# One more small TensorE product per item in the edge loop of a graph-attention and mixture-of-experts kernel

## What is computed

```python
def _L0_gnn_ref(feat, e_pro, mask, W_n, attn_l, attn_r, attn_m, src, dst):
    feat_src = (feat @ W_n).reshape(N, H, D)                 # H = 8 heads, D = 32
    el = jnp.einsum('nhd,hdt->nht', feat_src, attn_l)        # T = 4
    er = jnp.einsum('nhd,hdt->nht', feat_src, attn_r)
    em = jnp.einsum('ef,hft->eht', e_pro, attn_m)
    left = jnp.einsum('eht,et->eh', el[src], mask)
    right = jnp.einsum('eht,et->eh', er[dst], mask)
    em_e = jnp.einsum('eht,et->eh', em, mask)
    e = (left + right + em_e) / 3.0
    e = jnp.where(e > 0, e, NEG_SLOPE * e)
    ...
    e_exp = jnp.exp(e - e_max[dst])
    a = e_exp / e_sum[dst]
    msg = feat_src[src] * a[:, :, None]
    rst = jax.ops.segment_sum(msg, dst, num_segments=N)
```

## Time and profile before

| | |
|---|---|
| median of 3 runs | 4229.73 us (4228.48 to 4230.96) |
| the profiled execution | 4242.61 us, span 4240.8 us |
| TensorE matmul busy | 3155.8 us (74%) |
| TensorE weight loads busy | 2393.4 us (56%) |
| VectorE busy | 1982.3 us (47%) |
| ScalarE busy | 1615.5 us (38%) |
| GpSimd busy | 1861.5 us (44%) |
| granted TensorE clock, mean | 0.771 |

### The profile page before, as it was taken

How to read it: one execution, slowest core, us unless ns; L and a number is a source line. 1 busy time by engine, 2 the same in 40 slices (tenths; PEclk the granted TensorE clock), 3 DMA queues, 4 the chain that set the end, 5 groups by cost and what they waited for, 6 DMA issues and landing times. The chain is left out here.

```text
span 4240.8 us, 66247 instructions
## 1 busy us (share of the span) xinstructions
PE 3155.8 (74%) x12650; PEld 2393.4 (56%) x12651; DVE 1982.3 (47%) x5336; ACT 1615.5 (38%) x3611; POOL 1861.5 (44%) x1906
## 2 busy tenths in 40 slices
PE   2532787777777777777777777777766699999997
PEld 1221665555565656555555665565555477777775
DVE  5730555555555555555555555555744122222221
ACT  2311544444444444444444444444422122222221
POOL 0005455556555555555555555555245111111111
PEclk9865667777767777777777677767755899999998
DMA  7744444444444444444444444446553321221113
GB/s 217 253 134 120 122 128 124 125 127 126 125 125 127 128 123 127 131 128 126 125 127 124 125 125 125 125 125 118 87 176 133 101 32 30 32 31 31 31 31 82
DMA packets 311626, 480.40 MB, mean 113 GB/s; under 512 B 164215, under 2 KB 239811, under 8 KB 302670
## 3 DMA queue, kind: packets, MB, share of 16 engines
q0 software_dynamic: 100848, 285.40, 27.4%
q1 hardware_dynamic: 208606, 193.39, 15.2%
q10 hardware_dynamic: 2000, 0.06, 0.0%
HBM read 408.92 MB, written 76.12 MB: 114 GB/s over the span
## 5 line engine op out<-in xcount | busy, mean ns | idle before, releaser
L838 POOL DMA_INDIRECT rows<-table,idx x1664 | 1577.9, 948 | 1141.0 <-issue 488.8
L881 PE MATMUL ps_acc<-rows,hot 128*128 128x264 f32 x3328 | 1274.3, 521 | 396.9 <-DVE acc L1169 342.9
L881 PEld LDWEIGHTS ps_acc<-rows,hot 128*128 128x128 f32 x3328 | 767.9, 255 | 535.1 <-issue 422.0
L1169 DVE TENSOR_TENSOR acc<-acc,ps_acc 128x264 f32 x832 | 356.7, 429 | 1047.0 <-remote 459.5
L866 PEld LDWEIGHTS ps_term<-er,hot_t 128*128 128x128 f32 x3328 | 619.1, 249 | 285.6 <-issue 235.6
L866 PE MATMUL ps_term<-er,hot_t 128*128 x3328 | 608.2, 314 | 125.6 <-issue 93.3
L1155 DVE TENSOR_TENSOR rows<-rows,ps_p 128x512 f32<-128x512 f32 x832 | 565.7, 680 | 2.4 <-ACT ps_p L984 0.5
L973 ACT ACTIVATE hot<-iota_row,neg_rel 128x128 f32<-128x128 f32 x1664 | 545.8, 388 | 4.8 <-PE ps_acc L881 4.6
L1713 PE MATMUL ps_h<-w,acc 128*128 x1680 | 530.8, 459 | 0.5 <-ACT acc L1632 0.5
L1625 POOL DMA_INDIRECT x_dram<-acc,to x105 | 161.8, 1541 | 755.2 <-ACT acc L1641 755.2
L948 ACT COPY e_t<-ps_e 128x128 f32<-128x128 f32 x208 | 57.5, 277 | 1003.1 <-remote 684.3
(11 more groups left out here) (264 smaller groups left out, 2960.7 us busy)
## 6 DMA issues: line engine op xcount, KB each, us to landing
dst_row<-rel_d SPq DMA_DIRECT2D x52, 1024.0 KB
rows<-table,idx POOLq DMA_INDIRECT x1664
rec<-rec_d SPq DMA_DIRECT2D x848, 24.0 KB
rec_d<-acc SPq DMA_DIRECT2D x16, 1050.0 KB
acc<-slots_x SPq DMA_DIRECT2D x105, 130.0 KB, 2.1
acc<-in_edge_attr_dram SPq DMA_DIRECT2D x16, 700.0 KB
wrow<-in_L_ffn_w_dram SPq DMA_DIRECT2D x16, 640.0 KB
table<-fo SPq DMA_DIRECT2D x49, 148.0 KB
```

Of the source, the lines that this page charges most:

```text
L838: pool.indirect_dma_start(rows[w][:, t, :], None, table, bass.IndirectOffsetOnAxis(ap=idx[w][:, t:t + 1], axis=0)).then_inc(gathered[w * Q ...
L881: last = pe.matmul(ps_acc[m % 2][:, 0:PW], hot[m // QI % 2][:, m % QI * G + j, :], rows[m // NI][:, tile_of(m % NI, j), 0:PW], start=(j == ...
L1169: dve.tensor_tensor(so_far, so_far, ps_acc[m % 2][:, 0:PW].rearrange("p (h d) -> p h d", h=HEADS), ALU.add).then_inc(added, 1)
```

## The change

In sums, the wait for added comes first, and after it one more matmul is issued: 104 columns of the constant bm against the identity, into columns 264 to 367 of the item's bank, which nobody reads. Then come the waits for msg_ok and hot_ok and the two products as before, which write columns 0 to 263. The new matmul has no signal of its own. exp_ok is still waited for ahead of it.

```diff
+SPIN = 104
...
                         k1 = i * (2 * NI) + (at + 1)
                         if m % NI == 0:
                             pe.wait_ge(exp_ok, i * 2 + (at // NI + 1))
+
+                        after(pe, added, k1 - 2)
+                        pe.matmul(ps_acc[m % 2][:, PW:PW + SPIN], ident[:, :], flat(bm[:, :, :])[:, 0:SPIN], start=True, stop=True)
                         pe.wait_ge(msg_ok, k1)
                         pe.wait_ge(hot_ok, i * (2 * QUADS) + (at // QI + 1))
-
-                        after(pe, added, k1 - 2)
                         for j in range(G):
```

## The result

The changed kernel takes 4276.35 us (median of 4 runs, 4266.88 to 4277.6) against 4229.77 us before: 46.6 us more, a ratio of 1.0105 with the 95% interval 1.0089 to 1.0121. It is slower, and the forecast had it 18 us faster. The profiled execution took 4276.3 us, with a span of 4274.6.

What follows compares the result with a forecast made beforehand. The prediction took a ring of handshakes in the edge loop, with no engine full, to bound the kernel. Products at +66 us and the clock at -84 us gave net -18 us: 4211.7 us as a median, range 4120 to 4320.

Steps and rivals of the forecast that it cites:

- What bounds the kernel: In the edge loop no engine is full; a ring of handshakes, with TensorE's signals late while gathers stream, sets the pace.
- The moved wait at nothing: Before the sums in the edge loop, moving the wait for added ahead of msg_ok and hot_ok costs nothing by itself.
- The price of a product: On TensorE in the edge loop, each added product takes 0.22 us at full rate and 0.50 at half.
- The clock: In the edge loop TensorE's mean granted clock rises by 0.12, from 0.73 to 0.85, giving -84 us.
- The pass-through of 0.26: In the edge loop 0.26 of added TensorE time lengthens a turn; 253 us of products thus cost +66 us.
- 70 us for 0.10 of clock: Over the edge loop's 26 turns, a mean TensorE clock higher by 0.10 saves 70 us.
- Rival A: In the edge loop the clock rises to 0.99 and pays in full: -134 us, 4095.7 us; chance 0.10.
- Rival B: In the edge loop the clock stays at 0.73 and the products cost +80 us: 4309.7 us; chance 0.19.
- Rival C: In the edge loop a late sum signal makes GpSimd pause 2.78 us once a turn: +65 us, 4276.7 us; chance 0.17.
- Rival D: In the edge loop a clock gain of -63 us and product costs of +69 us nearly cancel: 4235.7 us; chance 0.18.
- Range and chances: For the whole kernel, 4120 to 4320 us; chances 0.46 faster, 0.18 the same, 0.36 slower.

## Why the prediction was wrong, point by point

**What bounds the kernel.** Right in that nothing is full and that the gathers of GpSimd pace the loop; its idle time before them grew from 1023.8 to 1041.3 us in 2500 us. That signals of TensorE are late because gathers are streaming, as the prediction put it, was not shown (last section).

**The moved wait at nothing.** Right (1.0001).

**The price of a product.** Right at half rate (0.53 us against 0.50), too low at full rate (0.28 us against 0.22). The prediction let the weight loads set the pace, as for few columns; 8 columns do take 0.22 us at full rate, 104 take more. At the measured clock of 0.78 this moves the mean from 0.343 to 0.391 us. The 356 ns of a pass of L880 are longer than that because passes overlap.

**The clock.** Mis-sized: +0.05 in place of +0.12. By the prediction's own prices this is the largest part of the miss, 49 of the 65 us between -18 and +46.6. The product comes behind the add, as the prediction said, so the silences remain, and the clock still falls to half rate: in the 24 turns of the changed kernel 22 idle stretches of TensorE are longer than 4 us, the granted clock just before them was 1.00, and after 20 of them TensorE resumed at half rate. Nor was 0.73 the lower bound of the mean, as the prediction had it: with 8 columns it fell to 0.61.

**The pass-through of 0.26, and 70 us for 0.10 of clock.** This is the step that failed in its mechanism. It came from five turns of one trace, and it took for a cause what only went along. The wait moved alone had a trace with more TensorE time a turn (79.7 us) and a lower clock (0.70) than the profile of before has over its 24 turns (76.9 us, 0.73), at 102.17 us a turn against 102.63; with 8 columns, 16.8 us more of TensorE cost 0.39 us. Inserted at 0.78, the formula gives 0.56 x 0.22 + 0.44 x 0.50 = 0.343 us, 832 x 0.343 x 0.26 = +74, less 0.5 x 70 = 35: +39 us, close to the 46.6 measured. That is no proof of it: with 0.70, the clock of the trace with the wait moved alone, in the place of before's 0.73, the same formula gives +18 us; the clock term measured 8 to 15 us for 0.10 (104 against 8 columns) and not 70; and the price of a product isn't even. Slower turns in the earlier trace rows had more TensorE time and a lower clock; that they were slower because of it was argued, and the runs speak against it. Repeated runs of the kernel before don't settle it: in one long sitting its 23 runs show no relation of time and clock, in a short one the longer of its 19 runs tend to have the lower clocks, and which follows from which can't be told.

**What the runs put in its place.** There is slack, and the slack has an end. In long sittings the ratios by products per batch are 1.0004 (4), 1.0006 and 1.0020 (8), 1.0032 (12, without the score quad), 1.0164 (12, without the items 0 to 3), 1.0105, 1.0097 and 1.0155 (16), 1.0104 (24, none in the score quad); in short ones 0.9989 (12), 1.0093 (16, behind all waits), 1.0213 (32). So a measurement of half of such a change would have called it free. In short sittings the loss goes with TensorE's busy time beyond the slack, and a product that delays its sum by 0.05 to 0.07 us instead of 0.28 to 0.53 is free (bfloat16, 1.0013). In long sittings, where the forecast was made and missed, busy time alone costs next to nothing (the wait moved alone, 8 against 104 columns), and the products cost what no single quantity read here explains. Why is open, and so is why the products of the score quad would need the others to become dear: its chain steps grow by the same 0.4 us where only its own products are there and nothing is lost.

**Rival A** fell with the clock. **Rival B**, the clock stays, was too strict: it rose by 0.05; the silences remained and the mean stayed below 0.8. The rule of the Trainium skill that an idle stretch of TensorE between bursts puts the clock back to half (TensorE: Matmul & The Clock Gate, HAM oscillation) agrees with that: it did so after 20 of the 22. But its price of 80 us rested on the same 0.26. **Rival C** named 4276.7 us, and 4276.35 came out. Its mark was there too, GpSimd's waits above 566 us although the clock rose, but it is no mark of the loss: with the products at the items 8 to 11 alone they are 605 us, and nothing is lost. Its place was not: the products at places 3 and 0 of a quad, which delay just the sum that it named, cost 0.20% alone. And its number was the sum of a clock gain that hardly exists (8 to 15 us for 0.10, as above) and a pause that was only supposed, so the agreement is an accident. **Rival D**, a wash at +0.09 of clock, rested on the same two prices; the clock rose by half of that, and 4276.35 us is 41 us above its 4235.7.

**Range and chances.** The time lay within the range of 4120 to 4320. The side was wrong: 0.46 was given to faster, 0.36 to slower. The range was 200 us wide, four times the loss, so that it holds the time says little.

## What to carry to other kernels

A raised clock is worth what the engine's time is worth, no more: find out first, with a run that makes the engine slower and changes as little else as possible, how much of that time reaches the end, and don't read it from turns of one trace that differ in several things at once. A filler behind the wait that ends an engine's idle time is not filler; it comes after the idle time and delays what was waited for. And in this ring of handshakes the prices of insertions did not add up: half of the change measured as free or nearly so, where the whole cost 1%.

## What the runs showed of the hardware that had not been expected

The kernel before took 4226 to 4243 us in three sittings and 3660 in two, a difference of 570 us or 13%, with unchanged code; the traces taken in the short sittings, all of changed kernels, lack the late signals. The waits of ScalarE before its copy of turned features and of GpSimd before its gathers, 500 to 2400 us: first before the change in a long sitting, then the kernel with the additional wait of GpSimd, equal to before in time, in a short one:

```profile
ACT e_t L948 <- remote: 532.4, 85, 7.8
...
POOL rows L838 <- PE ps_acc L881: 235.9, 146, 3.1
POOL rows L838 <- remote: 189.8, 76, 2.9
```
```profile
ACT e_t L953 <- PE ps_e L855: 397.5, 137, 6.8
...
POOL rows L843 <- PE ps_acc L886: 90.7, 162, 2.2
```

There is no "remote" wait on either engine in the second; ScalarE's wait is that for TensorE's product itself. Its 24 turns took 1980.12 us, 82.5 us each, against 102.6:

```profile
457.60:2437.72 1980.12, 1641.47 (x7250) 1342.39 (x7248) 1377.87 (x3499) 1174.53 (x2590) 1451.30 (x1536) 0.78 0.58 156
```

GpSimd's 64 gathers of a turn, with 0.95 us and a pause of 0.30 us each, make 80 us: in short sittings the loop runs nearly at the pace of its gathers. In long ones a turn takes 20 us more, and GpSimd's waits for TensorE, "remote" ones included, are 23 us a turn in place of 4. That the late signals cause all of this is argued, not shown. One chip was seen in both kinds, so the kind does not belong to the chip. What makes TensorE's signals late stays open. Streaming gathers alone don't: in the short sittings they stream more densely (156 against 125 GB/s in the rows of 24 turns), and no signal is late. The run that limits the gathers in flight fell into a short sitting.

The other surprise is the size of the effect of little on the clock: 8 columns in place of 104 in one small product per item took the loop's mean from 0.78 to 0.61 (in another long sitting), below the 0.73 and 0.70 of the traces without any product.
